# Sorting copies, evictions, gate chunks and weight loads in the class part, and the order of ScalarE's passes in the last phase, of an eight-core attention sandwich

## The reference, cut to what matters

```
x = x + layernorm(attn(layernorm(x)))        # x: 2 x 8192 x 1024
x = x + layernorm(ffn(layernorm(x)))
attn: q, k, v = x @ qkv_w.T + qkv_b          # 16 heads of 64
      for each of 44 offsets o (0..32, 48, 64, 96, ... 1536):
          logit_o = (q . k[n-o]) / 8 * (1 + q . scale_embed_o) + pos_bias_o
      p = softmax over the 44 offsets
      out = sum_o p_o * v[n-o] * if_gain
      out * sigmoid(x @ gate_w.T + gate_b) @ out_w.T + out_b
ffn:  complex linear map whose 1024 x 1024 matrix is built from small tensors G1, G2, plus a bias
```

## Time and profile before

| engine, core 7 | busy us | share of the span |
|---|---|---|
| PE (matmul) | 623.8 | 85% |
| DVE | 424.3 | 58% |
| ACT | 356.9 | 49% |
| POOL | 282.0 | 38% |

### The profile page before, as it was taken

One profiled execution on the slowest core, in us unless ns is written; L12 is line 12 of the kernel. 1 busy time (PEld: TensorE's weight loads), 2 busy tenths in 40 slices (PEclk: granted clock), 3 DMA queues, 4 the chain that ended last, 5 costly groups with the idle time before them and its releaser, 6 DMA issues.

```text
span 733.9 us, 15110 instructions; the slowest of 8 cores (719.2 to 733.9 us)
## 1 busy us (share of the span) xinstructions
PE 623.8 (85%) x5408; PEld 322.1 (44%) x5408; DVE 424.3 (58%) x782; ACT 356.9 (49%) x481; POOL 282.0 (38%) x303
## 2 busy tenths in 40 slices
PE   1599999999999999999877743889789999998773
PEld 0244455444445555555444422554345454444331
DVE  4365657222242777788558426654367776767762
ACT  3266665433334655565445633563455445454432
POOL 3388888300002413332028521243344545444210
PEclk9999999999999999999978986788688888889996
DMA  8857795985665699987684994594226555663111
GB/s 191 219 150 185 233 279 174 319 275 182 142 169 179 176 228 222 220 209 194 169 218 134 254 183 107 146 274 99 50 80 170 155 162 143 159 155 110 64 57 58
DMA packets 64833, 126.49 MB, mean 172 GB/s; under 512 B 26852, under 2 KB 29812, under 8 KB 64248
## 3 DMA queue, kind: packets, MB, share of 16 engines
q1 hardware_dynamic: 46152, 70.54, 36.0%
q0 software_dynamic: 12128, 40.20, 21.8%
q10 hardware_dynamic: 6480, 14.80, 5.5%
HBM read 85.39 MB, written 50.59 MB: 185 GB/s over the span
## 4 chain that ended last, share of the span: by engine, by line
PE 62%; DVE 14%; DMA 8%; issue 6%; ACT 6%; POOL 2%; SPq 1%; DVEq 0%; ACTq 0%; POOLq 0%
PE ps L307 25%; PE ps L336 14%; PE ps L816 9%; DMA rk<-pcimg 5%; PE ps L470 4%; DVE stt L253 3%; DMA rx<-xs 3%; PE ps L488 2%; PE ps L602 2%; DVE stt L254 2%; PE ps L281 2%; DVE rq L834 2%; PE ps L813 1%; PE ps L384 1%; ACT rx L873 1%
## 5 line engine op out<-in xcount | busy, mean ns | idle before, releaser
L307 PE MATMUL ps<-ry,rw 128*128 128x512 f16 x832 | 199.3, 394 | 2.4 <-DVE stt L270 1.9
L307 PEld LDWEIGHTS ps<-ry,rw 128*128 128x128 f16 x832 | 80.1, 101 | 97.9 <-issue 19.1
L602 PE MATMUL ps<-idb,rk 128*112 128x128 f16 x512 | 44.9, 246 | 49.5 <-DVE rk L365 31.8
L656 POOL TENSOR_SCALAR ry<-rx,cst 128x512 f16<-128x512 f32 x32 | 35.3, 1106 | 110.4 <-ACT rx L653 110.2
L336 PE MATMUL ps<-rw,ry 128*128 128x512 f16 x320 | 75.5, 380 | 0.0
L365 DVE CAST rs<-ps 128x896 f16<-128x896 f32 x32 | 34.8, 1091 | 67.2 <-PE ps L384 64.2
L816 PE MATMUL ps<-rw 128*128 128x512 f16 x256 | 71.9, 432 | 0.0
L816 PE MATMUL ps<-rq,rw 128*128 128x512 f16 x256 | 70.8, 427 | 0.0
L602 PEld LDWEIGHTS ps<-idb,rk 128*112 128x112 f16 x512 | 41.5, 154 | 60.5 <-issue 56.8
L881 POOL TENSOR_TENSOR rq<-rq,rx 128x1024 f32<-128x1024 f32 x14 | 32.8, 2346 | 73.4 <-ACT rx L873 59.4
L365 POOL COPY rk<-rk 128x896 f16<-128x896 f16 x28 | 50.8, 1822 | 24.7 <-PE ps L602 24.7
(11 more groups left out here) (112 smaller groups left out, 1057.8 us busy)
## 6 DMA issues: line engine op xcount, KB each, us to landing
rk<-vimg SPq DMA_DIRECT2D x64, 224.0 KB, 5.0
rx<-xs SPq DMA_DIRECT2D x21, 512.0 KB, 6.0
rq<-xs SPq DMA_DIRECT2D x16, 512.0 KB, 5.4
out<-rq SPq DMA_DIRECT2D x16, 512.0 KB, 2.8
plimg<-zt POOLq DMA_DIRECT2D x7, 1024.0 KB, 9.6
simg<-rs SPq DMA_DIRECT2D x32, 224.0 KB, 2.9
pcimg<-zt POOLq DMA_DIRECT2D x7, 1024.0 KB, 5.0
vimg<-rv ACTq DMA_DIRECT2D x28, 256.0 KB, 3.2
```

The lines of the kernel that those rows point to most:

```text
L307: mm = op("tensor", lambda e, ic=ic, wof=wof: e.matmul(ps[:, b * 512:(b + 1) * 512], w[:, wof:wof + 128], yt[:, yo + ic * 512:yo + (ic + 1 ...
L602: tp = op("tensor", lambda e, h=h: e.transpose(bass.AP(ph, b * 1024 + h * 128, [[8192, WK], [1, 128]]), sv(rk, PH + (hh * 8 + h) * WK, [1, ...
L656: gtok[g, oc] = thfree[s] = op("gpsimd", lambda e: e.tensor_scalar(dst, TH[s], hifg[:, oc:oc + 1], hifg[:, oc:oc + 1], ALU.mult, ALU.add), ...
```

## The change

- Start: token tiles 4, 5 and 6 wait for weight parts 1, 2 and 3 before they are loaded; the fourth weight part is issued directly behind the third; the G loads are issued in chunks 0 and 1 and wait for token tile 7.
- Class part: both halves of `class_sort` are on DVE and both evictions of `class_turn` on ACT (before, one half of each was on either). `g_next` takes 4, 4, 3 and then 1 a step (before 2, 1, 2, 1, ...); the total in the class part stays 24.
- The last three scatters move from POOL to SP, and `softmax_b` and `scatter` stand ahead of the class work of their step.
- `wbl` comes in two parts (w = 2, 3), `wol` in eight (w = 4 to 11).
- `bias_rows` moves to POOL with its loads, after w = 4, with three passes for each row where there were four.
- Last phase: the two `FO` passes (`d_fo`) stand behind the copy to XT and the second turn's eviction on ACT.

```diff
     def x_load(tt):
         if tt < NG * 4:
             xtok[tt] = dma("sync", f"xa{tt % 4}", XR[tt % 4],
-                           bass.AP(...), xfree[tt % 4])
+                           bass.AP(...), xfree[tt % 4],
+                           wkt.get(tt - 3) if tt > 3 else None)
...
     wkt[2] = w_part(rw0, "wk", 2)
-    for ri in range(2):
-        gts.append((dma("gpsimd", f"ga{ri}", ..., wkt[0]), dma("gpsimd", f"gb{ri}", ...)))
-        if ri == 0:
-            wkt[3] = w_part(rw0, "wk", 3)
+    wkt[3] = w_part(rw0, "wk", 3)
+    def g_load(ri, *waits):
+        gts.append((dma("gpsimd", f"ga{ri}", ..., *waits), dma("gpsimd", f"gb{ri}", ...)))
...
         mm = chunk(g, oc)
+        if n < 2:
+            g_load(n, xtok[7])
...
     def class_turn(U):
         b = qk_pair()
         p_turn(U, 0, b, "scalar")
-        p_turn(U, 1, b + 1, "vector")
+        p_turn(U, 1, b + 1, "scalar")
     def class_sort(U):
         p_sort(U, 0, "vector")
-        p_sort(U, 1, "scalar")
+        p_sort(U, 1, "vector")
...
     def bias_rows():
-        (DVE: memset rt, sel, sel; for each row: load on "sync", copy, subtract, subtract, multiply-add)
+        z = op("gpsimd", lambda e: e.memset(rt[:], 0.0), rsfree[0], rsfree[1], qsfree[3], qsfree[4])
+        a = op("gpsimd", lambda e: e.memset(sel[:], 0.0))
+        a = op("gpsimd", lambda e: e.memset(sel[0:2, :], 1.0), a)
+        for i, (nm, dst) in enumerate((("ob2", obr), ("fb2", fbr))):
+            b = XS[i][0:2, :]
+            ld = dma("gpsimd", f"br{i}", b, t[nm].ap(), lastqk)
+            a = op("gpsimd", lambda e, b=b: e.tensor_copy(hi, b), ld, a)
+            a = op("gpsimd", lambda e, b=b, d_=dst[0:2, :]: e.tensor_tensor(d_, b, hi, ALU.subtract), a, z)
+            a = op("gpsimd", lambda e, d_=dst[0:1, :]: e.tensor_copy(d_, hi[0:1, :]), a)
...
+        if s >= 16 and s - 3 in range(NU):       # ahead of the class work of step s
+            softmax_b(s - 3)
+            scatter(s - 3)                       # now always on "sync"
...
-            g_next(1)
+            g_next(4 if w < 2 else 3 if w == 2 else 1)
...
-            if w % 2 == 0:
-                g_next(1)
...
-            if w == 2:
-                wbl = dma("gpsimd", "wbl", wbig[:], ...)              # 8192 columns
-            if w == 6:
-                wol = dma("gpsimd", "wol", wo_[:, 0:8192], ...)
+            if w in (2, 3):
+                wbl = dma("gpsimd", "wbl", wbig[:, (w - 2) * 4096:(w - 1) * 4096], ...)
+            if 4 <= w < 12:
+                wol = dma("gpsimd", "wol", wo_[:, (w - 4) * 1024:(w - 3) * 1024], ...)
...
-        if s == 24:
+        if s == 20:
             bias_rows()
...
+    def d_fo(tt):                                # the two FO passes, before the end of d_fin2
...
         if s + 1 < NQ:
             p_turn(NU + s + 1, 1, 4, "scalar")
+        if old is not None:
+            d_fo(old)
```

More of the change, by code:

```diff
@@ L190, in build_program @@
     wkt[2] = w_part(rw0, "wk", 2)
-    for ri in range(2):
+    wkt[3] = w_part(rw0, "wk", 3)
+    def g_load(ri, *waits):
         gts.append((dma("gpsimd", f"ga{ri}", sv(rqf, GOFF[ri], [128, 4], [1, 128]),
-                        bass.AP(t["g1"], ri * 4 * 128 * 128, [[128, 128], [128 * 128, 4], [1, 128]]), wkt[0]),
+                        bass.AP(t["g1"], ri * 4 * 128 * 128, [[128, 128], [128 * 128, 4], [1, 128]]), *waits),
                     dma("gpsimd", f"gb{ri}", sv(rqf, GOFF[ri] + 512, [1, 64]), t["g2"].ap()[ri])))
-        if ri == 0:
-            wkt[3] = w_part(rw0, "wk", 3)
     zeros = []
@@ L548, in softmax_b, with scatter @@
         pdone[v] = op("vector", lambda e: e.tensor_tensor(po, ti, rb, ALU.mult), rz, scat.get(v - 2))
-    def scatter(v, eng):
+    def scatter(v):
         P_ = PP[v % 2]
-        sem = f"sc{eng[0]}{v % 2}"
+        sem = f"sc{v % 2}"
         for k in range(2):
             c = 2 * v + k
-            dma(eng, sem, bass.AP(t["plimg"], c * SKEW + 256, [[32 * SKEW, 64], [1, 528]]),
+            dma("sync", sem, bass.AP(t["plimg"], c * SKEW + 256, [[32 * SKEW, 64], [1, 528]]),
                 P_[k * 64:(k + 1) * 64, 0:528], pdone[v], zl[0])
-            dma(eng, sem, bass.AP(t["plimg"], c * SKEW, [[32 * SKEW, 64], [1, 16]]),
+            dma("sync", sem, bass.AP(t["plimg"], c * SKEW, [[32 * SKEW, 64], [1, 16]]),
                 P_[k * 64:(k + 1) * 64, 528:544])
         for s0, n, p0, st in CGROUPS:
-            scat[v] = dma(eng, sem,
+            scat[v] = dma("sync", sem,
                           bass.AP(t["pcimg"], v * 128 * SKEW + p0 * 16, [[SKEW, 128], [st * 16, n], [1, 16]]),
@@ L667, in bias_rows @@
     def bias_rows():
[L668 removed]
         hi = rs[0:2, 2048:3072]
[L670 to L680 removed]
+        z = op("gpsimd", lambda e: e.memset(rt[:], 0.0), rsfree[0], rsfree[1], qsfree[3], qsfree[4])
[7 more added lines that the diff above has]
+            a = op("gpsimd", lambda e, d_=dst[0:1, :]: e.tensor_copy(d_, hi[0:1, :]), a)
+        brt.append(a)
     gfree = {}
@@ L757, in build_program @@
             v_load(U)
-            if w == 2:
-                wbl = dma("gpsimd", "wbl", wbig[:], bass.AP(t["wbimg"], 0, [[8192, 128], [1, 8192]]),
+            if w in (2, 3):
+                wbl = dma("gpsimd", "wbl", wbig[:, (w - 2) * 4096:(w - 1) * 4096],
+                          bass.AP(t["wbimg"], (w - 2) * 4096, [[8192, 128], [1, 4096]]),
                           bank_v[0], wst["free"][0], wst["free"][1])
-            if w == 6:
-                wol = dma("gpsimd", "wol", wo_[:, 0:8192], t["wo"].ap(), lastqk)
+            if 4 <= w < 12:
+                wol = dma("gpsimd", "wol", wo_[:, (w - 4) * 1024:(w - 3) * 1024],
+                          bass.AP(t["wo"], (w - 4) * 1024, [[8192, 128], [1, 1024]]), lastqk)
         if s + 1 - 2 in range(NU):
             gather(s - 1)
-        if s - 3 in range(NU):
+        if s < 16 and s - 3 in range(NU):
             softmax_b(s - 3)
-            scatter(s - 3, "sync" if s < 16 else "gpsimd")
-        if s == 24:
+            scatter(s - 3)
+        if s == 20:
             bias_rows()
@@ L869, in d_fin2 @@
         m = op("vector", lambda e: e.tensor_scalar(sc(47), sc(47), -1.0, None, ALU.mult), m)
+        fom[tt] = m
+    def d_fo(tt):
+        src, m = ff_src(tt), fom[tt]
         for h in range(2):
@@ L874, in d_fin2 @@
                 m, fofree[tt % 2])
-    fofree, fot, mrg = [pdone[NU - 1]] * 2, {}, {}
+    fofree, fot, mrg, fom = [pdone[NU - 1]] * 2, {}, {}, {}
     def d_out(tt):
```

17 lines of the change are left out of this document (2 added, 15 removed).

## The result

The changed kernel takes **741.66 us** (median of 4 runs, 740.46 to 744.25); the kernel before, on the same chip, 734.17. The ratio is 1.0106, with an interval of 1.0073 to 1.0140: 1.1% slower, where 710 was forecast. In a later run of both it was 744.27 against 734.73, ratio 1.0125 (1.0081 to 1.0170). In some executions the cores of one die, or two of them, show a lower granted clock and a longer time: the medians and ratios here leave such executions out, and in the profiled execution of the kernel before cores 6 and 7 are such cores, at 0.82 in the last phase on core 7 where core 0 has 0.95.

What follows compares the result with a forecast made beforehand. PE was taken as the bound from 209 to 361 us (152 of 152 busy), with 43 us idle in the class part. 735.45 + 6 (start) - 21 (class part) - 10 (last phase) = 710.5; predicted 710 us, range 695 to 724.

Steps and rivals of the forecast that it cites:

- Start, +6: Start: G waits for tile 7, so POOL's chain begins near 36.5 us instead of 28.95; 6 us lost on core 7.
- the cover of one bank: Start, core 7: PE still had one of three banks at the eviction, so 6 us are lost; without cover, 8.6.
- An earlier or later first chunk changes nothing: Start: the time of PE's first chunk costs 0 us as long as POOL's chain is later.
- Gate chunks first, -9: Class part: five chunks moved into w = 0 to 4, where PE waits, save up to 1.8 us each; 9 us gained.
- scatters, +3: Class part: scatters on SP stand ahead of raw loads 0, 4 and 5; 3 us lost, bounds 0 to 14.
- The four early chunks cover most of it: Class part: early gate chunks hide most of the raw images' delay behind the scatters, leaving 3 us of up to 14.
- Bias rows, -11 and +5: Class part: PE's 11.3 us wait for DVE goes, 11 gained; some 20 us of work on POOL, partly covered, costs 5.
- Parts of the output weights, -7: Class part: output weights in eight parts hold raw images back less; 5 of 12 us spill, 7 gained.
- Engines, 0: Class part: sorting on DVE and evictions on ACT change nothing, 0 us; bound 0 to +5.
- Last phase, -10: Last phase: waits for XT go; 7 us from 13 steps and 2 to 3 from the tail, 10 gained.
- The second rival: Last phase: it gives nothing back, because d_ln's chain ends last; 720 us in all, chance 0.12.
- FO now ends when it did, so no bank is late: Last phase: FO behind the XT copy ends at its old time, so no bank is delayed; 0 us cost.

Runs made afterwards that it cites:

- e11_gearly: The changed kernel with the G loads early again, while tiles 4 to 6 still wait for weight parts: 741.01 us, ratio 1.0060 to the kernel before.
- r1: The changed kernel with the start, the gate chunks and the scatters with their softmax all as before: 729.41 us, ratio 0.9930 to the kernel before.
- e1_start: The changed kernel with the start as before, for both the tiles and the G loads: 735.99 us, ratio 1.0012 to the kernel before.
- e7_hoist: The changed kernel with raw images 0 and 1 ahead of the last scatters and softmax 14 and 15 ahead of the class work: 733.55 us, ratio 0.9988.
- e4_bias: The changed kernel with the bias rows back on VectorE, eight steps later, their small loads on SyncE: 753.68 us, ratio 1.0250 to the kernel before.
- r2: The kernel before with one part alone, the new bias rows on GpSimd at w = 4: 733.08 us, ratio 0.9975 to the kernel before.
- e6_parts: The changed kernel with FFN and output weights loaded whole again, at w = 2 and w = 6: 749.06 us, ratio 1.0177 to the kernel before.
- c4: c2 with the second sorting copy on ACT and the second eviction on VectorE, as before: 722.62 us, ratio 0.9820 to the kernel before.
- c2: The changed kernel with the old start, e7_hoist's order with V chunks first, a split wait in d_ln, weights early, bias rows late: 718.47 us, ratio 0.9764.
- e10_eng: The changed kernel with the class part's second sorting copy back on ACT and second turn's eviction on VectorE: 747.78 us, ratio 1.0168.

## Why the prediction was wrong

*Start, +6: +10.9.* The mechanism was right (chain, three chunks waiting), the size not: tile 7 let the first G load go out at 33.3 us on core 0 and 36.3 on core 1, and the four G issues and the landing took 4.7 us, not 3.5, so the chain began at 38.1 and 41.0 and not at 36.5. And the cover of one bank, which makes 6 us of 8.6, was core 7's: on four cores PE stood for the chain before. "An earlier or later first chunk changes nothing" holds only while the chain is later, as it says; with the chain early, e11_gearly still loses 6.7 us to its tiles.

*Gate chunks first, -9, and scatters, +3: together +4 to +6 (r1 against e1_start), 10 to 12 us off.* This is the step that failed in kind. "PE's idle time early is more than that, so I take the upper end" took any idle time for room. That idle time came from softmax 15 on VectorE and its exp on ACT, and a chunk needs ACT for its tanh, behind the same exp. Work that needs the engine that is held up can't fill the hole. "The four early chunks cover most of it" fell with it: the images behind the scatters came 10 us late, while DMA was at 0.42. With the border in another order (e7_hoist) the class part is 12.2 us shorter than before, near the -13 that the other terms make (-11 - 7 + 5).

*Bias rows, -11 and +5: -11 in the changed kernel (e4_bias), -2 alone (r2).* The 11.3 us on VectorE went. The chain tanh, eviction, PE was the prediction's own; I had counted 10 to 15 us of cover, from three steps. With one gate chunk a step, as in the changed kernel, the cover was enough (a tanh waited 2.6 us on core 1). With the old dealing, in r1 and r2, ACT, which works in order, stops at the first tanh without a buffer after some 5 us, with the evictions of the running steps behind it, and 12.6 to 13.5 us behind POOL took the place of what VectorE had won. The rows themselves took 21 us in r1, as estimated (20).

*Parts of the output weights, -7: about -5.6 (e6_parts)*, as far as the changed kernel shows it; right.

*Engines, 0: 2 to 4 us gained in the class part* (c4 against c2, within the noise; e10_eng); the sign that I had bounded the other way.

*Last phase, -10: -1.8 to -2.6.* The second rival was right (chance 0.12). The prediction had seen that PE waits for X2 already, and then let 7 us remain because a square root would start earlier. It did, by 0.5 us, and the product two passes later waited 0.6 us longer for GpSimd's copy. "FO now ends when it did, so no bank is late" stopped at the banks: GpSimd's sum and copy hang on FO and end when they did as well. The rule on the shared ports had been weighed for the class part alone. And the prediction didn't ask what the step is before and after: 12.3 us, a ring over VectorE, ACT and GpSimd. The last row, PE busy for 207 us, was that of a core at a low clock.

The sum closes by stages: +10.9 - 1.5 - 2.6 = +6.8, against 7.5 in the medians. The chances were wrong too: 0.04 for slower took the terms for independent, but r1, and e4_bias beside r2, show that they weren't.

## What to carry to other kernels

Before an idle stretch is filled, ask which in-order engine made it: only work that does not pass that engine can fill it, and an exp, a tanh and an eviction on one queue are one line of waiting. When a wait in a loop goes, compare the period of the loop, not the wait; the ring that sets it can lie on other engines, and a pass of 0.15 us can close it where it has to wait for another engine's copy. Undoing parts one at a time misleads when they come in pairs: undo the pair, or cut the time by stages on all cores first.
